# Softmax attention over eight-wide heads: four value tiles of 32 columns side by side, and exponentials over two PSUM banks

## The reference

```python
x = x + softmax_attention(layernorm(x))       # this study
x = x + local_attention_and_ffn_stack(layernorm(x))
x = x + linear_feature_attention(layernorm(x))
x = x + local_attention_and_ffn_stack(layernorm(x))

# softmax attention, T = 2048, 16 heads of d = 8
q, k, v = heads(x @ w_qkv); q = rope(q); k = rope(k)
scores = einsum('bhqd,bhkd->bhqk', q, k) / sqrt(8)
probs  = softmax(scores, axis=-1)
out    = einsum('bhqk,bhkd->bhqd', probs, v) @ w_out + b_out
```

## Time and profile before

| | |
|---|---|
| runs | 6148.74 us median of 3 (6134.6 to 6152.13) |
| span of the profiled execution | 6149.6 us; no other time of that execution is given |
| softmax attention, the 16 heads | about 138 to 1239 us |
| its projections, before and after | to 138 us, and 1239 to about 1250 us |
| the other layers | from about 1250 us on |
| TensorE, whole span | busy 5406.4 us (88%), granted clock 0.955 of full |

### The profile page before, as it was taken

One profiled execution on the slowest core, in us unless ns is written; L12 is line 12 of the kernel. 1 busy time (PEld: TensorE's weight loads), 2 busy tenths in 40 slices (PEclk: granted clock), 3 DMA queues, 4 the chain that ended last, 5 costly groups with the idle time before them and its releaser, 6 DMA issues. The chain is left out here.

```text
span 6149.6 us, 136606 instructions
## 1 busy us (share of the span) xinstructions
PE 5406.4 (88%) x39332; PEld 3486.8 (57%) x39332; DVE 4478.0 (73%) x8145; ACT 3905.8 (64%) x12160; POOL 2939.1 (48%) x2878
## 2 busy tenths in 40 slices
PE   5999999969899898998989956998989989899897
PEld 1222232246666666666666644666666666666665
DVE  7666666468688686886868844886868868688685
ACT  1555555647577575775757721775757757577575
POOL 2000000056566565665656612665656656566564
PEclk6999999989999999999999976999999999999999
DMA  0000000021222212122121211222222221222213
GB/s 12 1 1 1 1 1 1 1 80 46 73 51 58 60 46 72 48 60 60 46 72 46 62 47 56 50 58 61 50 67 51 58 61 48 70 51 58 61 46 87
DMA packets 332449, 288.38 MB, mean 47 GB/s; under 512 B 149246, under 2 KB 290852, under 8 KB 329892
## 3 DMA queue, kind: packets, MB, share of 16 engines
q1 hardware_dynamic: 331172, 282.34, 17.8%
q10 hardware_dynamic: 768, 0.02, 0.0%
HBM read 100.83 MB, written 30.41 MB: 21 GB/s over the span
## 5 line engine op out<-in xcount | busy, mean ns | idle before, releaser
L426 DVE TENSOR_REDUCE a_maxima<-a_bank 128x1 f32<-128x512 f32 x1024 | 677.7, 689 | 346.6 <-PE a_bank L541 342.7
L349 ACT ACTIVATE a_pex<-a_bank 128x512 f32<-128x512 f32 x1024 | 556.3, 596 | 415.3 <-PE a_bank L548 415.3
L1000 ACT ACTIVATE g_ex<-g_bank,g_nmx 128x96 f32<-128x96 f32 x1536 | 501.4, 338 | 345.4 <-DVE g_nmx L1082 345.4
L1000 ACT ACTIVATE f_ex<-f_bank,f_nmx 128x96 f32<-128x96 f32 x1536 | 501.4, 338 | 343.0 <-DVE f_nmx L1082 343.0
L935 POOL TENSOR_TENSOR f_rn<-f_sg,f_minus_half 128x8 f32<-128x8 f32 x384 | 640.2, 1667 | 32.0
L935 POOL TENSOR_TENSOR g_rn<-g_sg,g_minus_half 128x8 f32<-128x8 f32 x384 | 639.7, 1666 | 32.0
L940 POOL TENSOR_TENSOR f_qr<-f_t 128x512 f32<-128x512 f32 x384 | 547.6, 1426 | 14.8 <-DVE f_t L1101 13.1
L559 PE MATMUL a_bank<-a_pex,a_v_head 128*32 128x512 f32 x2048 | 544.3, 610 | 1.7 <-DVE a_osum L443 1.4
L940 POOL TENSOR_TENSOR g_qr<-g_t 128x512 f32<-128x512 f32 x384 | 537.3, 1399 | 14.8 <-DVE g_t L1101 13.1
L1177 PE MATMUL g_bank<-g_wqkv,g_xT 128*128 128x512 f32 x768 | 426.9, 639 | 87.4 <-DVE g_qh L1092 62.1
L1177 PE MATMUL f_bank<-f_wqkv,f_xT 128*128 128x512 f32 x768 | 427.1, 639 | 87.1 <-DVE f_qh L1092 61.8
(11 more groups left out here) (235 smaller groups left out, 13321.6 us busy)
## 6 DMA issues: line engine op xcount, KB each, us to landing
f_vw<-f_vt SPq DMA_DIRECT2D x96, 384.0 KB, 4.2
g_vw<-g_vt SPq DMA_DIRECT2D x96, 384.0 KB, 4.3
f_vw<-f_vt SPq DMA_DIRECT2D x96, 256.0 KB, 3.6
g_vw<-g_vt SPq DMA_DIRECT2D x96, 256.0 KB, 3.6
f_vw<-f_vt SPq DMA_DIRECT2D x96, 128.0 KB, 2.3
g_vw<-g_vt SPq DMA_DIRECT2D x96, 128.0 KB, 2.3
f_wqkv<-in_f_Wqkv_dram SPq DMA_DIRECT2D x7, 1536.0 KB, 7.7
g_wqkv<-in_f_Wqkv_dram SPq DMA_DIRECT2D x7, 1536.0 KB, 9.4
```

The costliest lines, as they stand in the source:

```text
L349: last = act.activation(pex[:, b, e, :], ps_s[2 * b + e][:], ACT.Exp)
L426: dve.tensor_reduce(maxima[:, m // 4, m % 4:m % 4 + 1], ps_max[m % 2][:], AX.X, ALU.max).then_inc(dv_max, 1)
L1000: last = act.activation(ex[:, b, u, :], ps_s[:, KEYS * u:KEYS * u + KEYS], ACT.Exp, bias=nmx[:, b, u:u + 1], accum_out=sm[:, b, u:u + 1])
```

## The change

The steps of a head are turned round. A step n of 32 now handles one key tile kt = n // 2 against two quarters of the queries (j = n % 2). Its two score matmuls share one stationary operand and fill one tensor `ps_s[j]` of two banks, and one ACTIVATE of 2 x 512 columns takes their exponential. `values(kt)` comes once per key tile, at the odd steps: four matmuls, one per quarter, with the same 32 columns of `v_head`, each on its own column tile, into its own partition group of `ps_o`; the sums run over all 16 key tiles there. So a head has one copy of `ps_o` instead of four, and in place of the 16 matmuls of `fold_sums` there are four transposes, `turn_sums`, at step 5. `outputs` reads the turned sums in their new order. The matrix `fold`, its load and its buffer go. The maxima keep their place: two to every step. FIRST and SECOND keep their steps (17, 19, 21, 23 and 29, 30 in the count of 32). The banks are allocated as two pairs and four single ones; `quarter` gives the single banks to the projections. The waits on `pe_pv` count calls of `values`, now 16 per head. Lines with only such renamed banks and other counts of `ld_c` are left out here.

```diff
-        banks = [ctx.enter_context(nc.psum_tensor(f"{tag}_bank{i}", [P, 512], F32)) for i in range(8)]
-        ps_max = banks[0:2]
-        ps_s = banks[2:6]
-        ps_o = banks[6]
-        ps_t = banks[7]
+        ps_s = [ctx.enter_context(nc.psum_tensor(f"{tag}_scores{i}", [P, 2, 512], F32)) for i in range(2)]
+        ps_max = [ctx.enter_context(nc.psum_tensor(f"{tag}_max{i}", [P, 512], F32)) for i in range(2)]
+        ps_o = ctx.enter_context(nc.psum_tensor(f"{tag}_sums", [P, 512], F32))
+        ps_t = ctx.enter_context(nc.psum_tensor(f"{tag}_turned", [P, 512], F32))
+        quarter = [ps_s[i // 2][:, i % 2, :] for i in range(4)]
...
-        pex = sb("pex", [P, 2, 2, GQ])
-        osum = sb("osum", [P, NG, GQ])
+        pex = sb("pex", [P, 2, NG, GQ])
+        osum = sb("osum", [P, GQ])
...
-        PASS, STEPS = 4 * NT, NT // 2 * NG
+        PASS, STEPS = 4 * NT, 2 * NT
...
-        FIRST = {(2, 1): 0, (2, 3): 1, (2, 5): 2, (2, 7): 3}
-        SECOND = {(3, 5): 0, (3, 6): 1}
-        FOLD, OUTPUT = (0, 3), (0, 4)
+        FIRST = {17: 0, 19: 1, 21: 2, 23: 3}
+        SECOND = {29: 0, 30: 1}
+        LAST, TURN, OUTPUT = 2, 5, 6
...
-            sp.dma_start(fold[:], consts["fold"]).then_inc(ld_c, 16)
...
-            pool.wait_ge(ld_c, 96)
+            pool.wait_ge(ld_c, 80)
...
-                    pool.wait_ge(pe_pv, STEPS * h + 2).then_inc(own["pool"], 1)
+                    pool.wait_ge(pe_pv, NT * h + 2).then_inc(own["pool"], 1)
...
-                for g in range(NG):
-                    for r in range(8):
-                        n = STEPS * h + (g * 8 + r)
-                        b = r % 2
-                        act.wait_ge(pe_s, n + 1)
-                        act.wait_ge(pe_pv, n + 1)
-                        for e in range(2):
-                            last = act.activation(pex[:, b, e, :], ps_s[2 * b + e][:], ACT.Exp)
-                        last.then_inc(act_ex, 1)
-                        if (g, r) in FIRST and exists(h, 2):
-                            first(h + 2, (u + 2) % 4, FIRST[g, r])
-                        if (g, r) in SECOND and exists(h, 1):
-                            second(h + 1, (u + 1) % 4, SECOND[g, r])
+                for n in range(STEPS):
+                    kt, j = n // 2, n % 2
+                    act.wait_ge(pe_s, STEPS * h + (n + 1))
+                    act.wait_ge(pe_pv, NT * h + (kt + 1))
+                    act.activation(pex[:, kt % 2, 2 * j:2 * j + 2, :], ps_s[j][:], ACT.Exp).then_inc(act_ex, 1)
+                    if n in FIRST and exists(h, 2):
+                        first(h + 2, (u + 2) % 4, FIRST[n])
+                    if n in SECOND and exists(h, 1):
+                        second(h + 1, (u + 1) % 4, SECOND[n])
...
-            def sums(h, g):
-                dve.wait_ge(pe_pv, STEPS * h + (8 * g + 10))
-                dve.tensor_copy(osum[:, g, :], ps_o[:]).then_inc(dv_os, 1)
+            def sums(h):
+                dve.wait_ge(pe_pv, NT * h + (NT + 2))
+                dve.tensor_copy(osum[:], ps_o[:]).then_inc(dv_os, 1)
             def outputs(h):
+
                 dve.wait_ge(pe_f, h + 1)
-                both = ps_t[:, 0:NT * VW].rearrange("p (t c) -> p t c", t=NT)
-                dve.reciprocal(rec[:], both[:, :, AD]).then_inc(dv_rec, 1)
+                both = ps_t[:].rearrange("p (s g c) -> p g s c", s=GT, g=NG)
+                by_tile = rec[:].rearrange("p (g s) -> p g s", g=NG)
+                dve.reciprocal(by_tile, both[:, :, :, AD]).then_inc(dv_rec, 1)
                 dve.wait_ge(dv_rec, h + 1)
                 at = ao[:, :, h * AD:h * AD + AD] if isinstance(h, int) else ao[:, :, bass.ds(h * AD, AD)]
-                dve.tensor_tensor(at, both[:, :, 0:AD], rec[:].unsqueeze(2).broadcast_to([P, NT, AD]), ALU.mult).then_inc(dv_ao, 1)
+                dve.tensor_tensor(at.rearrange("p (g s) d -> p g s d", g=NG), both[:, :, :, 0:AD],
+                                  by_tile.unsqueeze(3).broadcast_to([P, NG, GT, AD]), ALU.mult).then_inc(dv_ao, 1)
...
-                for g in range(NG):
-                    for r in range(8):
-                        if r == 1 and (g or exists(h, -1)):
-                            if g:
-                                sums(h, g - 1)
-                            else:
-                                sums(h - 1, NG - 1)
-                        if g * 8 + r == LATE and exists(h, 1):
-                            negate(h + 1, (u + 1) % 2)
-                        ahead, which = carried(g * 8 + r)
-                        if exists(h, ahead):
-                            for m in which:
-                                maximum(h + ahead, m)
-                        if (g, r) == OUTPUT and exists(h, -1):
-                            outputs(h - 1)
+                for n in range(STEPS):
+                    if n == LAST and exists(h, -1):
+                        sums(h - 1)
+                    if n == LATE and exists(h, 1):
+                        negate(h + 1, (u + 1) % 2)
+                    ahead, which = carried(n)
+                    if exists(h, ahead):
+                        for m in which:
+                            maximum(h + ahead, m)
+                    if n == OUTPUT and exists(h, -1):
+                        outputs(h - 1)
...
-            def scores(h, slot, g, r):
-                pe.wait_ge(act_ex, STEPS * h + (g * 8 + r + 1))
+            def scores(h, slot, n):
+
+                kt, j = n // 2, n % 2
+                pe.wait_ge(act_ex, STEPS * h + (n + 1))
                 for e in range(2):
-                    kt = 2 * r + e
-                    last = pe.matmul(ps_s[2 * (r % 2) + e][:], stackT[:, slot, 1, P * kt:P * kt + P],
+                    g = 2 * j + e
+                    last = pe.matmul(ps_s[j][:, e, :], stackT[:, slot, 1, P * kt:P * kt + P],
                                      stackT[:, slot, 0, GQ * g:GQ * g + GQ], start=True, stop=True)
                 last.then_inc(pe_s, 1)
-            def values(h, p, g, r):
-                pe.wait_ge(act_ex, STEPS * h + (g * 8 + r + 3))
-                if r == 0:
-                    pe.wait_ge(dv_os, NG * h + (g + 1))
-                for e in range(2):
-                    kt = 2 * r + e
-                    c = 32 * (kt % 4)
-                    last = pe.matmul(ps_o[c:c + VW, :], v_head[:, p, kt, :], pex[:, r % 2, e, :], start=(kt < 4), stop=(kt >= 12),
-                                     tile_position=(0, c))
+            def values(h, p, kt):
+
+                pe.wait_ge(act_ex, STEPS * h + (2 * kt + 4))
+                if kt == 0:
+                    pe.wait_ge(dv_os, h + 1)
+                for g in range(NG):
+                    last = pe.matmul(ps_o[VW * g:VW * g + VW, :], v_head[:, p, kt, :], pex[:, kt % 2, g, :],
+                                     start=(kt == 0), stop=(kt == NT - 1), tile_position=(0, VW * g))
                 last.then_inc(pe_pv, 1)
-            def fold_sums(h):
-
-                pe.wait_ge(dv_os, NG * h + (NG + 1))
+            def turn_sums(h):
+
+                pe.wait_ge(dv_os, h + 2)
                 if exists(h, 1):
                     pe.wait_ge(act_second, 2 * h + 4)
-                for t in range(NT):
-                    last = pe.matmul(ps_t[:, VW * t:VW * t + VW], osum[:, t // GT, P * (t % GT):P * (t % GT) + P], fold[:],
-                                     start=True, stop=True)
+                for t in range(GT):
+                    last = pe.transpose(ps_t[:, P * t:P * t + P], osum[:, P * t:P * t + P], ident[:])
                 last.then_inc(pe_f, 1)
             def head(h, u):
                 pe.wait_ge(act_second, 2 * h + 2)
                 pe.wait_ge(pl_vh, h + 1)
-                for g in range(NG):
-                    for r in range(8):
-                        ahead, which = carried(g * 8 + r)
-                        if exists(h, ahead):
-                            if which[0] == 0:
-                                pe.wait_ge(act_first, 4 * h + 12)
-                            scores_for_max(h + ahead, (u + ahead) % 4, which[0])
-                        scores(h, u % 4, g, r)
-                        if exists(h, ahead):
-                            scores_for_max(h + ahead, (u + ahead) % 4, which[1])
-
-                        if r:
-                            values(h, u % 2, g, r - 1)
-                        elif g:
-                            values(h, u % 2, g - 1, 7)
-                        elif exists(h, -1):
-                            values(h - 1, (u + 1) % 2, NG - 1, 7)
-                        if (g, r) == FOLD and exists(h, -1):
-                            fold_sums(h - 1)
-                        if (g, r) in FIRST and exists(h, 2):
-                            first(h + 2, u % 2, FIRST[g, r])
-                        if (g, r) in SECOND and exists(h, 1):
-                            second(h + 1, (u + 1) % 2, SECOND[g, r])
+                for n in range(STEPS):
+                    ahead, which = carried(n)
```

(44 more changed lines are left out.)

## The result

The changed kernel takes 5904.54 us (median of 4 runs, 5901.95 to 5907.18) against 6148.95 us before: a ratio of 0.9604, 95% interval 0.9591 to 0.9618. The forecast was 5900 us. The medians are 244.4 us apart; the profiled execution spans 5900.1 us, 249.5 less than the profiled one before.

The account below looks back on a forecast made before the run. It took the order and length of TensorE's work to bound the attention stage. Savings of 182.5, 18.4, 50 and 11 less 13 made 249 us: 6149.6 to 5900.6, predicted 5900, with an 8-in-10 range of 5870 to 6020.

Parts of the forecast that it names:

- Values and stall: Attention steps carrying maxima: fewer value calls, less a 0.29 us wait for DVE; a pair takes 3.13 us, not 3.90, saving 182.5.
- c: First maximum matmul of a pair's odd step; claimed to start at 1.17 us instead of 0.88, waiting for DVE's reduction.
- Exponentials: ACT's softmax exponentials: one of 1024 columns takes 1.02 us, hidden behind TensorE while maxima are carried.
- Pairs without maxima: The 19 pairs of steps carrying no maxima: 2.07 us each instead of 3.04, 18.4 us less in all.
- ACT's chain: Scores, two exponentials and the waiting matmul in pairs without maxima: 4.14 us for two pairs, longer than TensorE alone.
- Folds: End-of-head summing matmuls replaced by four transposes of 0.49 us: 3.1 us less, 16 times, 50 us.
- Clock: Granted clock falling after the folds in 7 of the first 15 heads: 1.6 us each, 11 us regained.
- Dearer parts: Costs added in 14 heads: negation 8 us, copy of the sums 3.5, second transposes 1.5; 13 us together.
- second transposes: Second group of SECOND's stack transposes, waiting for ACT's copy: 0.1 us above 0.45 a group, 1.5 us over 14 heads.
- two at a time: Rival on value calls: only two streams run together whatever the tile, four rounds a call; 6129 us, chance 0.08.
- slowed: Rival on value calls: four tiles run together but each round takes 0.68 us for 0.45; 6015 us, chance 0.09.
- The clock's rival: Rival: TensorE's 0.29 us waits halve the granted clock, 5.5 us a pair; 6500 us if in all pairs; chance 0.04.

## Why the prediction was right

By its own steps, from the profiled executions; the forecast stands in brackets.

- *Values and stall.* A pair is 3.142 us (3.13), 0.763 less than 3.905: 237 pairs give 180.8 (182.5). Four rounds of two tiles became two rounds of four, and a call of two rounds is as long on four tiles as on two, within 0.02 us. c's 1.17 and the stall of 0.29 are on the timeline, and the kernel with half reductions takes 0.26 of the 0.29 away.
- *Exponentials.* 1.026 us (1.02), hidden: in the old order by the kernel with that part alone, ratio 1.0002; in the new one TensorE's value matmuls wait for ACT 0.6 us in all.
- *Pairs without maxima.* 2.08 us each over two pairs (2.07), 18.1 (18.4). That is over the 1.95 that TensorE alone would need, as forecast from ACT's chain; no run tests that chain by itself.
- *Folds.* Transposes 0.48 to 0.50 us (0.49); 3.1 less in 16 heads, 49.6 (50).
- *Clock.* This term was too good: 7.5 (11). No fall is left behind the sums. But the loop's two back edges, where the program jumps back and TensorE stands idle, cost it 1.9 us each before and cost 2.0 and 2.5 now, and behind them the granted clock now falls from 1.00 to 0.50, for 1.7 and 1.4 us more. The two falls, and the 4 us around the first of them beside ordinary ones:

```profile
413.90:417.30 3.40, 3.39 (x12) 0.50 0.00 0
635.80:639.10 3.30, 3.30 (x14) 0.50 0.01 2
412.00:416.00 4.00, 3.12 (x12) 0.73 0.03 8
488.00:492.00 4.00, 3.86 (x26) 1.00 0.01 2
```

In the kernel before, the 4 us behind its first back edge keep the full clock:

```profile
484.06:488.06 4.00, 4.00 (x17) 1.00 0.03 8
```

- *Dearer parts.* Negation 0.72 to 0.73 in its pair (0.75), copy of the sums 0.31 (0.25), second transposes 0.55 (0.55): together 13.1 (13). For the negation the prediction took 0.57 over today's 0.2, where its own 0.75 gives 0.55; it measured 0.53.

The measured terms add up: 180.8 + 18.1 + 49.6 + 7.5 - 13.1 = 242.9, and the last division comes 242.6 us earlier. The forecast for it was 249, 6 too much, 3.5 of them from the clock and 1.7 from the pairs. The profiled span is nonetheless 249.5 shorter. The other 7 us lie behind the last division, in layers that the change does not touch: that stretch takes 4911 us before and 4904 in the changed kernel, and 4896 to 4913 in the traces of the experiments. So that the profiled span meets 5900 is luck; the medians, 244.4 us apart, lie within 2 us of what the terms give.

The rivals: "two at a time" and "slowed" are refuted by the three kernels on fewer tiles, and by the two windows in a call. "Slowed" had 0.45 us more per call, and a call of two rounds is 0.02 us longer on four tiles than on two. The clock's rival did not come about in the pairs: 0.99 over the heads, with 0.29 us of waiting in each pair. Of its kind are only the two falls behind the back edges. The stall for DVE, which the new order uncovered, is 237 x 0.29 = 69 us of the 250 that the pairs would give without the stall.

## What to carry to other kernels

Before forecasting a gain from packing more matmuls together, find out from one timeline how many rounds a call has and what surrounds it: here the rounds, the way in (0.31 us from the matmul before) and the way out (0.15 us beyond the rounds, an estimate: 1.00 less two rounds of 0.425) were separate prices, and with the rounds of the earlier trace rows they could be read off the old trace. A block of work that is made twice as long half as often can uncover what it used to hide, here 0.29 us in each of 237 pairs; write down, for each double-buffered resource, when its release comes against the new order, and do the same again for every reordering that is meant to cure it, with the neighbour's work in the queue counted in. The negation's six short dependent instructions left TensorE idle for 1.50 us when they stood in a row on DVE, and for 0.17 with reductions between them; so nearly all of what such a row costs can be its waits, and other work between them is worth a try.

## What the runs showed of the hardware that was not expected

- TensorE started a matmul on a free column tile past an earlier one that waited for a busy tile: with two matmuls for one tile ahead of two for the other, two instructions were at work from 503.04 on, where the call on one tile alone had one at work in its first 0.42 us, and the call took 1.92 us, against 1.91 in alternating order.
- The first round of a call took 0.45 us and each further one 0.42 to 0.43, with one tile at work or two (3.62 us for eight rounds on one, 1.91 for four on two); two rounds took 1.07 us on four tiles and 1.05 on two.
- The granted clock fell from 1.00 to 0.50 behind a stretch of 3.76 us of small fp32 matmuls in some heads and not in others of the same execution (8 of 15 in one), and behind idle time of 1.95 and 2.40 us at a loop's back edges in the changed kernel, where it had not fallen behind 1.82 us in the kernel before. What decides it was not settled.
